# A message-passing layer on one core: the sums of routed groups taken after two of every three of them, a ring handed out tile by tile, and SyncE's loads in a written order

## The reference, cut to what matters

```
h    = x @ W_in2f                                        # 6250 x 128
Wij  = (ssp(edge_attr_20 @ W_filt1 + b_filt1) @ W_filt2 + b_filt2) * edge_weight
x_ij = h[dst] * Wij                                      # 200000 x 128
agg  = segment_sum(x_ij, src, 6250)                      # src is in no order
out  = ssp(agg @ W_out1 + b_out1) @ W_out2 + b_out2
x    = layernorm(x + out)                                # ssp(v) = softplus(v) - ln 2
```

## Time and profile before

| | us |
|---|---|
| median of three runs (lowest, highest) | 2171.71 (2170.34, 2175.63) |
| the profiled execution's own time | 2169.02 |
| its span, from the first to the last instruction | 2167.3 |

### The profile page before, as it was taken

One profiled execution on the slowest core, in us unless ns is written; L12 is line 12 of the kernel. 1 busy time (PEld: TensorE's weight loads), 2 busy tenths in 40 slices (PEclk: granted clock), 3 DMA queues, 4 the chain that ended last, 5 costly groups with the idle time before them and its releaser, 6 DMA issues.

```text
span 2167.3 us, 52608 instructions
## 1 busy us (share of the span) xinstructions
PE 2039.4 (94%) x16433; PEld 1713.0 (79%) x16433; DVE 1943.3 (90%) x4035; ACT 1587.9 (73%) x3852; POOL 1700.0 (78%) x1038
## 2 busy tenths in 40 slices
PE   2589999999999999999999999999999999999946
PEld 2468888888888888888888888888888888888823
DVE  6669999999999999999999999999999999999847
ACT  0278777777777777777877777777778777778617
POOL 2048888888888888888888888888888888888864
PEclk8689999999999999999999999999999999999978
DMA  9546656656656656566566565665665665666584
GB/s 328 200 86 94 103 92 102 103 83 107 101 87 105 98 96 104 88 103 103 82 108 99 92 106 91 102 102 84 103 102 83 107 99 88 106 94 87 83 210 131
DMA packets 346333, 235.22 MB, mean 109 GB/s; under 512 B 86087, under 2 KB 325554, under 8 KB 345850
## 3 DMA queue, kind: packets, MB, share of 16 engines
q0 software_dynamic: 140976, 64.22, 32.1%
q1 hardware_dynamic: 194598, 150.79, 27.0%
q10 hardware_dynamic: 10476, 16.77, 2.1%
HBM read 145.44 MB, written 86.20 MB: 107 GB/s over the span
## 4 chain that ended last, share of the span: by engine, by line
PE 33%; DMA 25%; issue 15%; POOL 14%; DVE 10%; ACT 3%; DVEq 0%; ACTq 0%; POOLq 0%; SPq 0%
DMA table<-total,index 23%; POOL table L714 13%; PE unit_psum L1670 9%; PE unit_psum L1689 7%; PE both_psum L1627 6%; PE total_psum L1640 4%; PE pre_psum L1608 3%; PE both_psum L1652 2%; DVE scat_hot L1325 1%; DVE route_hot L1308 1%; DVE hidden L1246 1%; PE both_psum L1623 1%; DVE same L1226 1%; DMA b_o<-in_b_o 1%; DVE acc_t L1342 1%
## 5 line engine op out<-in xcount | busy, mean ns | idle before, releaser
L714 POOL DMA_INDIRECT table<-total,index x979 | 1641.3, 1676 | 410.5 <-issue 242.9
L1670 PE MATMUL unit_psum<-moving,route_hot 128*128 128x258 f32 x4088 | 656.9, 298 | 2.0 <-DVE acc_t L1342 1.4
L892 ACT ACTIVATE ring<-unit_psum 128x258 fp32r<-128x258 f32 x1022 | 389.5, 399 | 299.8 <-PE unit_psum L1670 280.9
L1670 PEld LDWEIGHTS unit_psum<-moving,route_hot 128*128 128x128 f32 x4088 | 534.5, 189 | 62.3 <-ACT ring L892 42.4
L1689 PE MATMUL unit_psum<-scat_hot,ring 64*128 64x448 f32 x4088 | 459.2, 371 | 10.5 <-DVE scat_hot L1325 9.5
L1325 DVE TENSOR_SCALAR scat_hot<-node_iota,ring 128x448 fp32r<-128x448 uint16 x1022 | 461.4, 465 | 0.8 <-ACT ring L892 0.7
L869 ACT ACTIVATE h_dst<-both_psum,edge_cols 128x128 f32<-128x128 f32 x1564 | 451.5, 388 | 7.3 <-DVE message L1272 2.4
L1689 PEld LDWEIGHTS unit_psum<-scat_hot,ring 64*128 64x128 f32 x4088 | 376.3, 185 | 86.3 <-ACT ring L892 37.8
L1308 DVE TENSOR_SCALAR route_hot<-node_iota,slot_cols 128x896 fp32r<-128x896 uint16 x584 | 395.1, 703 | 37.3 <-PE unit_psum L1670 37.3
L1627 PE MATMUL both_psum<-w_f,hidden 128*128 128x128 f32 x3128 | 425.7, 279 | 0.0
L1627 PEld LDWEIGHTS both_psum<-w_f,hidden 128*128 128x128 f32 x3128 | 400.5, 193 | 21.5 <-issue 16.2
(11 more groups left out here) (124 smaller groups left out, 1574.3 us busy)
## 6 DMA issues: line engine op xcount, KB each, us to landing
dst_b<-dst SPq DMA_DIRECT2D x391, 128.0 KB
src_b<-src SPq DMA_DIRECT2D x245, 128.0 KB
f_t<-in_f_t SPq DMA_DIRECT2D x98, 256.0 KB, 4.4
table<-total,index POOLq DMA_INDIRECT x979
table<-zeros ACTq DMA_DIRECT2D x20, 640.0 KB, 10.1
window<-h_parts SPq DMA_DIRECT2D x391, 32.0 KB
parts<-table SPq DMA_DIRECT2D x48, 256.0 KB, 5.0
h_parts<-h_out SPq DMA_DIRECT2D x12, 384.0 KB, 2.8
```

What stands on the lines that cost most here:

```text
L714: pool.indirect_dma_start(tables[k], bass.IndirectOffsetOnAxis(index[:, i, k:k + 1], 0), total[:, i, k, 0:DIM], None, compute_op=ALU.add). ...
L892: act.activation(ring[:, r[1] % RING, k, :], unit_psum[:, k % 2, 0:MOVING], ACT.Copy).then_inc(ring_done, 1)
L1670: last = pe.matmul(unit_psum[:, k % 2, 0:MOVING], route_hot[:, tile, k * P:(k + 1) * P], moving[:, tile, :], start=(tile == 0), stop=(tile ...
```

## The change

1. **Places.** The routed groups are at places 2, 4 and 7 of a period (before 1, 4 and 6), the last two at 386 and 388 (before 385 and 388). There are still 146, and 245 plain ones.
2. **Steps.** A step of sums follows only the first and the third of three routed groups (`STEPS_AT`). Step s takes slot tile s % 7 of all groups routed since step s - 7: 10 or 11 in place of 7. There are 104 steps in place of 152, with the same 1,022 sums and 208 adds in place of 304. `rest()` holds 58 sums and 23 route tiles in place of 42 and 20.
3. **Ring.** Each slot tile gets a place from a list of free ones (`place_in_ring`); a place is free once its tile has been summed. 44 places in place of 49. The one-hots of `slot_one_hot` have 7 buffers used in turn (`HOTS`): the n-th waits for the sum n - 7, whatever the step.
4. **Waits.** Where no step lies between two routed groups, the first two tiles of the second wait for ScalarE's copies of the last two of the first, and no longer for adds.
5. **Orders.** The orders of ScalarE, VectorE and TensorE are written anew. SyncE gets `unit` and `rest` too, in place of one step per group.

```diff
-ROUTED_AT = (1, 4, 6)
+ROUTED_AT = (2, 4, 7)
-LAST_ROUTED = (385, 388)
+LAST_ROUTED = (386, 388)
+STEPS_AT = (0, 2)
-RING = SLOT_TILES
+HOTS = 7
+def step_route(n):
+    return n // len(STEPS_AT) * len(ROUTED_AT) + STEPS_AT[n % len(STEPS_AT)]
+def taken(s, x):
+    if not 0 <= s[1] < STEPS:
+        return None
+    r = step_route(s[1] - SLOT_TILES) + 1 + x
+    oldest = NEWEST[s[1] - SLOT_TILES] + 1 if s[1] >= SLOT_TILES else 0
+    return (s[0], r) if oldest <= r <= NEWEST[s[1]] else None
...
 # keep_slots
-                if taken(m, 0) is not None and k == 0:
-                    act.wait_ge(taken_done, through_taken(m, 0))
-                act.activation(ring[:, r[1] % RING, k, :], unit_psum[:, k % 2, 0:MOVING], ACT.Copy
+                if (r[1], k) in FREED_BY:
+                    act.wait_ge(taken_done, FREED_BY[r[1], k])
+                act.activation(ring[:, RING_AT[r[1], k], :], unit_psum[:, k % 2, 0:MOVING], ACT.Copy).then_inc(ring_done, 1)
 # slot_one_hot
+                n = through_taken(s, x)
+                if n > HOTS:
+                    dve.wait_ge(taken_done, n - HOTS)
 # VectorE's unit(u), up to make_index of group 1
+                mark_repeated(g(-3), plain)
+                make_index(g(-3), plain)
                 multiply(g(0), plain)
+                route_one_hot(r(-1), 0); route_one_hot(r(-1), 1); route_one_hot(r(-1), 2)
...
+                mark_repeated(g(-2), plain)
+                compare_dst(g(4))
+                make_index(g(-2), plain)
                 mark_repeated(g(0), plain)
                 make_index(g(0), plain)
                 multiply(g(2), plain)
                 finish_hidden(pair(2))
...
+                slot_one_hot(s(-1), 7); slot_one_hot(s(-1), 8)
+                multiply(g(3), plain)
+                slot_one_hot(s(-1), 9)
+                route_one_hot(r(0), 2)
+                slot_one_hot(s(-1), 10)
                 split_lo(r(0))
+                mark_repeated(g(1), plain)
...
+                add_slice(s(-1), 0); add_slice(s(-1), 1)
                 multiply(g(4), plain)
+                make_index(g(1), plain)
 # route
-                elif first_taken(m) is not None:
-                    pe.wait_ge(acc_done, through_adds(m, k))
+                elif r[1] - 1 in STEP_AFTER:
+                    pe.wait_ge(acc_done, through_adds((0, STEP_AFTER[r[1] - 1]), k))
+                elif r[1] > 0:
+                    pe.wait_ge(ring_done, through_tile(plus(r, -1), SLOT_TILES - 1 - k))
 # TensorE's unit(u)
+                route(r(-2), 5)
+                gather(g(2))
+                route(r(-2), 6)
+                sum_repeated(g(-2), plain)
                 first_layer(pair(2))
                 second_layer(g(1))
                 sum_repeated(g(0), plain)
+                route(r(-1), 0); route(r(-1), 1)
+                second_layer(g(2))
+                route(r(-1), 2); route(r(-1), 3)
                 gather(g(3))
+                route(r(-1), 4)
+                sum_repeated(g(1), plain)
+                route(r(-1), 5); route(r(-1), 6)
+                gather(g(4))
                 first_layer(pair(3))
                 second_layer(g(3))
+                sum_slots(s(-1), x) for x = 0 to 10, one by one
+                gather(g(5))
                 second_layer(g(4))
                 sum_repeated(g(3), plain)
+                route(r(0), 0); route(r(0), 1)
                 gather(g(6))
+                route(r(0), 2); route(r(0), 3)
                 first_layer(pair(4))
+                gather(g(7))
+                route(r(0), 4)
                 second_layer(g(5))
+                route(r(0), 5); route(r(0), 6)
                 second_layer(g(6))
+                sum_slots(s(0), x) for x = 0 to 6, one by one
                 sum_repeated(g(5), plain)
                 gather(g(8))
                 first_layer(pair(5))
+                sum_slots(s(0), 7); sum_slots(s(0), 8); sum_slots(s(0), 9)
+                second_layer(g(7))
+                route(r(1), 0); route(r(1), 1)
                 gather(g(9))
+                route(r(1), 2); route(r(1), 3)
                 second_layer(g(8))
+                route(r(1), 4)
 # SyncE's unit(u), the second half
+                next_window(g(11)); next_window(g(12))
+                next_features(quad(7))
+                next_src(g(11), plain)
+                next_dst(g(12)); next_dst(g(13))
...
```

More of the change, by code:

```diff
@@ L192, in through_tile @@
     return SLOT_TILES * r[1] + k + 1
[L195 to L217, removed]
@@ L220, in first_taken, with newest_routes @@
[L220 to L229, removed]
+def step_route(n):
+    return n // len(STEPS_AT) * len(ROUTED_AT) + STEPS_AT[n % len(STEPS_AT)]
+def newest_routes():
+    newest = []
+    while len(newest) < SLOT_TILES or newest[-SLOT_TILES] < ROUTES - 1:
+        newest.append(min(ROUTES - 1, step_route(len(newest))))
+    return newest
@@ new lines, with through_taken, place_in_ring @@
+TAKEN_BEFORE = [0]
+for n in range(STEPS):
+    TAKEN_BEFORE.append(TAKEN_BEFORE[-1] + len(places_taken((0, n))))
+def through_taken(s, x):
+    return TAKEN_BEFORE[s[1]] + (x - places_taken(s)[0] + 1)
+def place_in_ring():
+    free, tiles, where, freed_by, last = [], 0, {}, {}, {}
+    s = 0
+    for r in range(ROUTES):
+        for k in range(SLOT_TILES):
+            if not free:
+                free.append(tiles)
+                tiles += 1
+            where[r, k] = free.pop(0)
+            if where[r, k] in last:
+                freed_by[r, k] = last[where[r, k]]
+        while s < STEPS and NEWEST[s] == r:
+            for x in places_taken((0, s)):
+                tile = where[taken((0, s), x)[1], s % SLOT_TILES]
+                free.append(tile)
+                last[tile] = through_taken((0, s), x)
+            s += 1
+    return tiles, where, freed_by
@@ L641, in _ @@
             with sp.If(is_narrow):
-                run_single(step_narrow)
+                for k in range(2):
+                    sp.wait_ge(h_stored[k], 16 * (FULL_CHUNKS // 2 + (k == 0)))
+                run_periods(unit, rest)
                 sp.wait_ge(route_mm_done, through_tile((0, ROUTES - 1), SLOT_TILES - 1))
@@ L1419, in rest @@
                 multiply((0, 384), plain)
-                slot_one_hot((0, 145), 4); slot_one_hot((0, 145), 5)
-                compare_src((0, 387), plain); compare_src((0, 389), plain)
-                compare_dst((0, 389))
+                mark_repeated((0, 381), plain)
+                compare_dst((0, 387))
+                make_index((0, 381), plain)
+                compare_dst((0, 388))
+                route_one_hot((0, 143), 0); route_one_hot((0, 143), 1); route_one_hot((0, 143), 2)
+                split_lo((0, 143))
@@ new lines, in rest @@
+                route_one_hot((0, 143), 3)
+                mark_repeated((0, 382), plain)
+                compare_dst((0, 389))
+                make_index((0, 382), plain)
+                multiply((0, 385), plain)
+                mark_repeated((0, 384), plain)
+                make_index((0, 384), plain)
+                finish_hidden((0, 194))
+                compare_src((0, 389), plain)
+                multiply((0, 386), plain)
+                compare_src((0, 390), plain)
+                compare_dst((0, 390))
@@ L1440, in rest @@
[L1440 to L1447 removed]
+                finish_hidden((0, 195))
+                add_slice((0, 95), 0); add_slice((0, 95), 1)
+                mark_repeated((0, 385), plain)
@@ L1654, in gather, with route @@
                 last.then_inc(gather_done, 1)
[L1656 to L1658 removed]
+            def route(r, k):
                 if not routes(r):
@@ L1689, in sum_slots @@
                         last = pe.matmul(unit_psum[:, strip, 0:BUCKET],
-                                         ring[rows, r[1] % RING, slot_tile(m), part * DIM:(part + 1) * DIM],
-                                         scat_hot[rows, r[1] % RING, :], start=first and part == 0,
+                                         ring[rows, RING_AT[r[1], slot_tile(s)], part * DIM:(part + 1) * DIM],
+                                         scat_hot[rows, (n - 1) % HOTS, :], start=first and part == 0,
                                          stop=final and part == 1)
```

474 lines of the change are left out of this document (223 added, 251 removed).

## The result

The changed kernel takes 2207.2 us (median of 4, 2202.8 to 2213.7) where the kernel before takes 2173.7 beside it (2170.3 to 2182.7): a ratio of 1.015 (95% interval 1.011 to 1.019). It is slower by 1.5%, and 7 us above the top of my range. The profiled span grew from 2167.3 to 2205.5 us, by 38.2.

What follows compares the result with a forecast made beforehand. GpSimd's undrained scatter queue was taken as the bound, close to TensorE's pace. Scatters -4, start +4 and end +3 gave +3 on the profiled 2169.0, so 2172; the median lies 2.7 higher, hence 2174 us, range 2139 to 2200.

Steps and rivals of the forecast that it cites:

- Waits added: One-hots on VectorE waiting for sum n - 7 in the run of 11: counted as nothing, up to 0.5 us a period.
- A: GpSimd's never-drained scatter queue sets the pace at 39.4 to 39.8 us a period: 2160 to 2186 us; chance 0.45.
- TensorE's content: Same matmuls on TensorE, but the row of six route tiles is broken up: its period falls 0.6 us to 38.9.
- Adds: 96 fewer adds on VectorE, 58.6 us of its time or 1.2 us a period: counted at nothing.
- Scatters: 979 scatters on GpSimd as before, period 39.6 against 39.69 us over 46 periods: -4 us.
- Start: At the kernel's start, later indices make GpSimd's queue fill 4 us later (0 to 7).
- End: After the last period: 9.6 us of TensorE work moved there, 6 us back by running ahead; net +3 us (-3 to +9).
- Ring: A ring place is freed by a step lying before the group that takes it: nothing either way.
- SyncE: New load order gains nothing; `compare_src` may be late at a unit's end, 0 to 0.5 us a period of VectorE's slack.
- Rival C: ScalarE's `copy_total` stuck waiting for landed scatters, 40 to 40.3 us a period: 2192 to 2206 us; chance 0.22.
- Rival D: New TensorE stall at the long run of sums or first route tiles behind it, 0.5 to 1 us a period; chance 0.05.

## Why the prediction was wrong

The step that failed is "Waits added", as I put it: "Behind it on VectorE stand `split_lo` and the adds, which the next route tiles want about 2 us later. I take nothing". The first half of it held: one-hot 10 at 4.0 us into the run, forecast 4.6 at the latest. But I had not counted the queue to its end. Between `split_lo` and the adds stand a `moved`, three one-hots of the next slot tile and a `route_one_hot`, 2.0 us from the end of `split_lo` (1012.46) to the adds; and the wait for the eighth buffer lasts until the first sum has been taken, 0.79 us into the run, not 0.5. With 0.61 us for one add (an estimate, the mean of the adds in the profile), the first add ends 7.2 us into the run, and the route tile begins at 7.3; it could have started at 6.8. It came to 0.83 us a period by buffers (40.58 less the 39.75 of nine; 0.72 in the even stretch, 40.46 less 39.74), above the "up to 0.5" that I allowed. That it is more than the half microsecond at this place, because what stands behind the adds on VectorE is late as well, is argued and not shown place by place.

Point by point:

- *GpSimd's queue as the pace* (my forecast, A): wrong for the new kernel, small for the old (0.29 us a period). I had set one period of TensorE (39.49) against the mean of 46 of GpSimd (39.69) and called the first steady; over the even stretch both have 39.62. (Twenty times 1.84 us is 36.8, not 36.9; nothing hangs on it.)
- *TensorE's content, -0.6 us*: right in size for the matmuls that go, -0.57 within stretches, but I said that the changes of operation "cost the same". Even with nine buffers they cost 0.65 more, so TensorE's own period isn't 38.9 us but 39.73 in the even stretch with GpSimd relieved as well; the old order so relieved has 39.43.
- *Adds at nothing*: too low. Cutting a third of them in the old kernel was worth 0.6%, by a way that stays open. Whether the 96 adds that the change removes are what the kernel with nine buffers gains wasn't separated.
- *Scatters, -4*: the pace was +40.9. Their mean rose to 1.714 us, but relieving them moved the new kernel by 0.3% only.
- *Start +4*: it was -4.1. *End +3*: +1.4; the last scatter ends (2112.95) 5.1 us ahead of the last adds (2118.06), forecast 4.
- *Ring and SyncE at nothing*: nothing found; the old order of loads is no faster.
- *Rival C*: landings did hold `copy_total` 20 times, three of them long enough to stall TensorE, with a fall of its clock behind each that I had not reckoned with; at most some 15 us. The slow period is there without them. *Rival D*, which I gave 0.05, is the right mechanism in the right place, "the first route tiles behind it"; the profiled period is 0.9 us above GpSimd's 39.7, within its 0.5 to 1, and its range, 2185 to 2210, holds the time. That range was too low for its own price, though: 46 x 0.5 to 1 on A's 2174 are 2197 to 2220.

## What to carry over

When a run that takes buffers grows (7 sums to 11) and the buffers stay at 7, don't ask only if the run itself is fed. Write out the producer's queue behind the first held instruction, to the last item that anyone wants, with each one's length. Here two more buffers of 1792 bytes a partition, in memory that the ring's smaller size (44 tiles for 49) had freed, turn a change that costs 1.5% into one that gains 0.4% (2167.5 us against 2177.6 before, interval 0.9943 to 0.9978); this is the version to keep.

An engine that is 90% busy and "sets no period" isn't free: in a ring of engines with short buffers between them, 1.3 us of standing still on it came out as 0.7 to 0.8 us of period.

## What was not expected of the hardware

What surprised was mostly the schedule. Two things of the chip are worth keeping. The first is the clock: at the end of each of the three long stalls, 2.0 to 3.0 us without a matmul, TensorE's granted clock fell from 1.00 to 0.50, and it was busy again for some us at that level. There eight matmuls of the repeated sums took 1.84 us where they take 1.06 at 1.00, so a short stall costs more than its own length.

The second: with a fourth of the scatters gone, those left took longer on the mean in the kernel before (1.740 against 1.676 us). I put this down to their beginning when their index comes, right beside VectorE's work, which isn't shown:

```profile
L715 POOL DMA_INDIRECT table<-total,index x735 | 1279.3, 1740 | 751.7 <-DVE index L1292 468.8
```

The same cut took the mean from 1.680 to 1.747 us with nine buffers, and from 1.714 to 1.706 with seven. A scatter's mean time is thus not a constant to take over from one order into another.
